# A conv-attention and mixture-of-experts kernel: one tap spread for all images, and tn made twice instead of stored

## The reference, cut to what matters

```python
# 1. attention weights from a 7x7 convolution (dilation 2) of the normalised image
k = relu(conv(ln_c(x), w1, dilation=2, padding=6) + b1)
attn = softmax(relu(batchnorm(conv1x1(k, w2) + b2)), axis=1)       # 49 taps per pixel
# 2. attend: each pixel is the weighted sum of its 49 neighbours, the same for all channels
x = x + sum(attn[:, p] * shifted(ln_c(x), p) for p in range(49))
# 3. a mixture of experts on the tokens t of x, routed by image
t = tokens(x); tn = layernorm(t)
w, i = top2(routing(mean(tn, axis=1)))                              # two of eight experts per image
y = sum(w[k] * (gelu(tn @ W1[i[k]] + b1) @ W2[i[k]] + b2) for k in 2)
out = t + layernorm(y + tn) * gamma + beta
```

## Time and profile before

| | us |
|---|---|
| median of three runs | 1263.26 (1258.61 to 1263.72) |
| profiled execution | 1263.83 |
| its span | 1261.9 |
| PE busy | 1128.5 (89%) |
| PEld busy | 981.5 (78%) |
| DVE busy | 714.7 (57%) |
| ACT busy | 494.8 (39%) |
| POOL busy | 236.2 (19%) |
| mean granted clock of PE | 0.896 |
| DMA | 106.34 MB, 84 GB/s |

### The profile page before, as it was taken

One profiled execution on the slowest core, in us unless ns is written; L12 is line 12 of the kernel. 1 busy time (PEld: TensorE's weight loads), 2 busy tenths in 40 slices (PEclk: granted clock), 3 DMA queues, 4 the chain that ended last, 5 costly groups with the idle time before them and its releaser, 6 DMA issues. The chain is left out here.

```text
span 1261.9 us, 19335 instructions
## 1 busy us (share of the span) xinstructions
PE 1128.5 (89%) x7380; PEld 981.5 (78%) x7380; DVE 714.7 (57%) x1719; ACT 494.8 (39%) x923; POOL 236.2 (19%) x160
## 2 busy tenths in 40 slices
PE   4788999999999999578779887699899989989997
PEld 3776666666667665378779887699899989989997
DVE  3554453554454252335754674667677667777676
ACT  4573323323322110132543443645545535445442
POOL 1000000000000000100440462213233222232332
PEclk9788999999999999556775785799999989999999
DMA  9311121022020000233990685423124221421211
GB/s 256 106 38 38 38 75 39 1 86 80 1 65 27 1 12 4 52 85 86 253 270 3 169 244 177 130 71 107 50 76 126 70 70 50 137 75 42 71 51 38
DMA packets 98968, 106.34 MB, mean 84 GB/s; under 512 B 5298, under 2 KB 95699, under 8 KB 98692
## 3 DMA queue, kind: packets, MB, share of 16 engines
q1 hardware_dynamic: 79888, 86.15, 24.0%
q10 hardware_dynamic: 19000, 19.11, 5.0%
HBM read 65.69 MB, written 39.56 MB: 83 GB/s over the span
## 5 line engine op out<-in xcount | busy, mean ns | idle before, releaser
L706 PE MATMUL pM<-V,U 128*128 128x368 f16 (+3 forms) x2016 | 320.9, 316 | 0.0
L706 PEld LDWEIGHTS pM<-V,U 128*128 128x128 f16 x2016 | 197.3, 98 | 108.2 <-issue 1.6
L1473 DVE TENSOR_TENSOR gl<-gf,gh 128x384 fp32r<-128x384 f32 x192 | 161.8, 864 | 63.4 <-ACT gh L1367 63.4
L1367 ACT ACTIVATE gf<-pH,b1c 128x384 f32<-128x384 f32 x192 | 112.1, 584 | 195.3 <-PE pH L1586 146.3
L1601 PE MATMUL pY<-w2h,gh 128*128 128x256 f32 x576 | 168.6, 293 | 17.3 <-DVE z L1485 16.4
L1601 PE MATMUL pY<-w2l,gh 128*128 128x256 f32 x576 | 164.1, 285 | 0.0
L1601 PE MATMUL pY<-w2h,gl 128*128 128x256 f32 x576 | 164.0, 285 | 0.0
L510 DVE TENSOR_TENSOR V<-pV,V 128x384 f16<-128x384 f32 x96 | 53.1, 554 | 164.9 <-ACT V L408 164.9
L1586 PE MATMUL pH<-xh,w1h 128*128 128x384 f32 x384 | 131.7, 343 | 8.5 <-DVE w1l L1444 4.2
L1586 PE MATMUL pH<-xl,w1h 128*128 128x384 f32 x384 | 131.2, 342 | 0.0
L1586 PE MATMUL pH<-xh,w1l 128*128 128x384 f32 x384 | 131.0, 341 | 0.0
(11 more groups left out here) (173 smaller groups left out, 1544.7 us busy)
## 6 DMA issues: line engine op xcount, KB each, us to landing
xa<-in_xt SPq DMA_DIRECT2D x16, 576.0 KB, 4.9
xn_scratch<-xa SPq DMA_DIRECT2D x16, 576.0 KB, 5.9
xn<-xn_scratch SPq DMA_DIRECT2D x16, 576.0 KB, 8.7
xr<-in_xt SPq DMA_DIRECT2D x16, 576.0 KB, 6.8
t_scratch<-ts ACTq DMA_DIRECT2D x16, 576.0 KB, 5.6
tn_scratch<-tn ACTq DMA_DIRECT2D x16, 576.0 KB, 5.2
tnk<-tn_scratch SPq DMA_DIRECT2D x24, 384.0 KB, 3.3
tk<-t_scratch SPq DMA_DIRECT2D x24, 384.0 KB, 3.9
```

What stands on the lines that cost most here:

```text
L706: return nc.tensor.matmul(out[:, :, first:end], U[:, hi_u, k, piece, :], V[:, b % 2, hi_v, k, c, :, first + TILES * d:end + TILES * d], st ...
L1367: last = nc.scalar.activation(dst, pH[:, j % 4, 0:CN], ACT.Gelu, bias=b1c[:, j // FB, j % FB:j % FB + 1])
L1473: tt(gl[:, sl, j, :], gf[:, j % 2, :], gh[:, sl, j, :].bitcast(F32), ALU.subtract).then_inc(g_step, 1)
```

## The change

Attend is rebuilt. Blocks are five rows of the image instead of four (`BROWS`; `TB` = 120 tokens, five blocks, the last of 96), which makes 13 (t, d) pairs x 3 = 39 matmuls an image. High and low taps are stacked on 98 partitions, and one spread fills A for all 16 images: 11 (d, h) pairs x 4 slots of six matmuls, each with 80 columns (64 where h = 4). The bank holds the sum of both halves: ACT copies it to A's high half, DVE subtracts that to get the low half. X has three buffers, tn isn't stored, and the order on DVE, ACT and SP is another. In the FFN only t is loaded (six buffers, four chunks ahead), and tn is made again: `statistics` on DVE, `scale_x` on POOL, `normalise` on ACT.

```diff
+BROWS = 5
+TB = BROWS * SIDE
+HHS = [(d, h) for d in (-1, 0, 1) for h in range(BROWS) if h - R < BROWS * (d + 1) and h + R >= BROWS * d]
+SLOT = 6
+XB = 3
+SBANKS, OBANKS = 3, 4
...
-        aT = sb("aT", [TAPS, 2, GI * PIX], F16)
-        A = sb("A", [TT, BLK, 2 * BT, TT], F16)
+        aT = sb("aT", [2 * TAPS, N], F16)
+        A = sb("A", [TB, BLK, 2, IMGS, NB, TB], F16)
...
 (SP, attend; halves() cuts each transfer in two: four blocks of 120, one of 96)
             def load_x(n):
                 if n >= 2:
                     sp.wait_ge(t_step, (n - 2) * T_STEPS + T_SUMS)
-                sp.dma_start(xr[:, n % 2], src).then_inc(xr_loaded[n % 2], 16)
+                for src, dst in halves(xt, n, xr[:, n % 2]):
+                    sp.dma_start(dst, src).then_inc(xr_loaded[n % 2], 16)
+            for hl in range(2):
+                sp.dma_start(aT[hl * TAPS:(hl + 1) * TAPS, :], attn_d[:, hl, :]).then_inc(at_loaded, 16)
...
+            for n in range(2, IMGS):
+                load_xn(n)
+                load_x(n)
...
 (POOL, attend)
+            for a in range(2):
+                nc.gpsimd.memset(A[:, 0, a, :, :, R * SIDE:TB], 0.0).then_inc(a_zeroed, 1)
+                nc.gpsimd.memset(A[:, 2, a, :, :, 0:(BROWS - R) * SIDE], 0.0).then_inc(a_zeroed, 1)
...
 (ACT, attend)
+            def store(n):
+                act.wait_ge(t_step, n * T_STEPS + T_SUMS)
+                for dst, src in halves(t_d, n, ts_[:, n % 2]):
+                    act.dma_start(dst, src).then_inc(t_stored[n % 2], 16)
-                act.dma_start(tn_d[rows, :].rearrange("(t p) c -> p t c", p=TT),
-                              tn[:, n % 2]).then_inc(tn_stored[n % 2], 16)
+            for u in range(NU):
+                act.wait_ge(spread, u + 1)
+                nc.scalar.copy(spread_to(0, u), spread_from(u)).then_inc(ahi_spread, 1)
+                if u in (NU // 3, 2 * NU // 3):
+                    x_high(u // (NU // 3) - 1)
             for n in range(IMGS):
+                if n + 2 < IMGS:
                     x_high(n + 2)
                 if n > 0:
+                    store(n - 1)
                     normalise(n - 1)
-                    store(n - 1)
...
 (DVE, attend)
+            for u in range(NU):
+                dve.wait_ge(ahi_spread, u + 1)
+                nc.vector.tensor_tensor(spread_to(1, u), spread_from(u), spread_to(0, u), ALU.subtract).then_inc(alo_spread, 1)
             for n in range(IMGS):
+                if n + 2 < IMGS:
+                    x_low(n + 2)
                 sums(n)
-                if (n + 1) % GI > 0:
-                    statistics(n)
-                    if n + 2 < IMGS:
-                        x_low(n + 2)
+                statistics(n)
...
 (PE, attend)
+                if u >= SBANKS:
+                    pe.wait_ge(alo_spread, u - SBANKS + 1)
+                for w in range(k * SLOT, (k + 1) * SLOT):
...
+                    last = nc.tensor.matmul(pS[0:TB, u % SBANKS, o:o + IMGS * nb], G[:, v, at:at + TB],
+                                            aTv[:, :, first:first + (nb - 1) * TB + 1:TB], start=True, stop=True)
...
 (FFN)
+TBUFS = CHUNKS
+X_STEPS = 2 * CT + 2
+AHEAD = 4
...
-                sp.dma_start(tnk[:, s], tn_d[rows, :].rearrange("(t p) c -> p t c", p=P)).then_inc(tnk_loaded[s], 16)
...
 (POOL, FFN: in step m scale_x(m+3) stands ahead of add_bias(m+1))
+            def scale_x(b, m):
+                n, s = CHUNKS * b + m, m % 2
+                pool.wait_ge(x_step, (n + 1) * X_STEPS)
+                if not (is_first(b) and m < 2):
+                    pool.wait_ge(tn_made, 2 * (n - 1))
+                nc.gpsimd.tensor_tensor(xrs[:, s], xve[:, s], mhalf[:, :], ALU.pow).then_inc(x_scaled, 1)
+                pool.wait_ge(x_scaled, 2 * n + 1)
+                nc.gpsimd.tensor_tensor(xsh[:, s], xnm[:, s], xrs[:, s], ALU.mult).then_inc(x_scaled, 1)
...
 (ACT, FFN: in step m normalise(m+3) stands between gelus(m+1) and take_x(m+2))
+            def normalise(b, m):
+                n, s = CHUNKS * b + m, m % 2
+                act.wait_ge(x_scaled, 2 * (n + 1))
+                if not (is_first(b) and m < 2):
+                    act.wait_ge(x_turned, 2 * (n - 1))
+                    act.wait_ge(bias_added, 2 * (n - 1))
+                for t in range(CT):
+                    last = nc.scalar.activation(tnk[:, s, t, :], tk[:, m % TBUFS, t, :], ACT.Identity,
+                                                bias=xsh[:, s, t:t + 1], scale=xrs[:, s, t:t + 1])
+                last.then_inc(tn_made, 2)
...
+            normalise(0, 0)
+            normalise(0, 1)
             take_x(0, 0)
...
 (DVE, FFN: in step m statistics(m+3) stands ahead of everything else)
+            def statistics(b, m):
...
+                for t in range(CT):
+                    s.did(nc.vector.bn_stats(xst[:, t, :], tk[:, m % TBUFS, t, :]))
...
+                for t in range(CT):
+                    s.did(nc.vector.bn_aggr(xmv[:, t, :], xst[:, t, :]))
...
+                s.did(nc.vector.tensor_scalar(xve[:, sl], xmv[:, :, 1], 1e-5, None, ALU.add))
+                s.did(nc.vector.tensor_scalar(xnm[:, sl], xmv[:, :, 0], -1.0, None, ALU.mult))
```

More of the change, by code:

```diff
@@ L955, in _, with spread_to, spread_from @@
                 scale(n)
-                if n % BI != 1 and 0 < n <= IMGS - LATE:
+                if n % BI != 1 and n > 0:
                     accumulate(n - 1)
[L959 to L972, removed]
+            accumulate(IMGS - 1)
+        def spread_to(hl, u):
+            d, h, k = ITEMS[u]
+            at = h * SIDE + k * SLOT
+            return A[:, d + 1, hl, :, 0:blocks_of(h), at:at + SLOT]
+        def spread_from(u):
+            nb = blocks_of(ITEMS[u][1])
+            return pS[0:TB, u % SBANKS, 0:SLOT * IMGS * nb].rearrange("p (w n t) -> p n t w", w=SLOT, t=nb)
         @block.scalar
@@ L986, in normalise @@
                 if n >= 2:
-                    act.wait_ge(tn_stored[n % 2], 16 * (n // 2))
                     act.wait_ge(acc_step, summed(n - 2))
[L990 to L993, removed]
-                last.then_inc(tn_ready, 1)
[L996 to L1000, removed]
-                act.dma_start(tn_d[rows, :].rearrange("(t p) c -> p t c", p=TT),
-                              tn[:, n % 2]).then_inc(tn_stored[n % 2], 16)
+                else:
+                    act.wait_ge(pads_set, 4 + n)
@@ new lines, in normalise @@
+                for t in range(NB):
+                    rows = rows_of(t)
+                    last = nc.scalar.activation(tn[0:rows, n % 2, t, :], ts_[0:rows, n % 2, t, :], ACT.Identity,
+                                                bias=shift[0:rows, n % 2, t:t + 1],
+                                                scale=rstd[0:rows, n % 2, t:t + 1])
+                last.then_inc(tn_ready, 1)
+            for u in range(NU):
[3 more added lines that the diff above has]
+                    x_high(u // (NU // 3) - 1)
@@ L1042, in statistics @@
                 s.settle()
-                for t in range(NT):
-                    s.did(nc.vector.bn_stats(st[:, t, :], ts_[:, n % 2, t, :]))
+                for t in range(NB):
+                    rows = rows_of(t)
+                    s.did(nc.vector.bn_stats(st[0:rows, t, :], ts_[0:rows, n % 2, t, :]))
                 s.settle()
-                for t in range(NT):
-                    s.did(nc.vector.bn_aggr(mv[:, t, :], st[:, t, :]))
+                for t in range(NB):
+                    rows = rows_of(t)
+                    s.did(nc.vector.bn_aggr(mv[0:rows, t, :], st[0:rows, t, :]))
                 s.settle()
@@ L1527, in body @@
                 for m in range(CHUNKS):
+                    if later(b, m, 3, CHUNKS):
+                        statistics(*later(b, m, 3, CHUNKS))
                     if m == 0 and not is_first(b):
```

310 lines of the change are left out of this document (159 added, 151 removed).

## The result

The changed kernel took 1342.72 us (median of four runs, 1335.85 to 1344.74) against 1260.93 us before (four runs, 1256.41 to 1263.72): a ratio of 1.0643, with a 95% interval of 1.0588 to 1.0698. It is slower by 82 us. The forecast was 1379, with a range of 1300 to 1420. The profiled execution took 1340.77 us, its span is 1339.0 us and its mean granted clock 0.881.

A forecast was written before the change was run, and what follows sets the result against it. It took attend as seemingly bound by bytes, the FFN chunk by PE and the DVE/ACT chain. Terms: 1263.8 + 4 (attend) + 5 (FFN head) + 71 (chunk waits) + 35 (clock) = 1379 us; range 1300 to 1420.

The forecast's parts named there:

- The sign: Whole kernel: slower by over 0.5%, chance 0.89; within 0.5%, 0.04; faster, 0.07.
- the clock holds: Rival, FFN: PE's waits do not lower its clock, total 1344 us (band 1330 to 1350); chance 0.17.
- Head of attend: Attend's start until the first spread matmul: 22.5 us, 9 longer than the 13.5 before, for the larger load.
- The case at the upper end: Attend's head: both tap transfers of 49 rows share seven DMA engines, 2.4 us more than the 9 taken.
- Spread: Spread of the taps: 264 matmuls at 0.173 us at the low clock, 47 us with the last copies, 35 saved.
- Ring: Attend loop: xn load, x_high, x_low and sums wait in a closed circle, 12.2 us an image, 13 turns, 159 us.
- the ring gives back what was saved: Attend: the closed ring eats what spread and stores save, so the stage ends 4 us later, at 786.5.
- bytes decide: Rival, attend: bytes, not order, set 7.2 us an image, 65 us less; FFN chunks add nothing; 1208 us; faster, chance 0.07.
- FFN head: Start of the FFN: tn must be made before the first layer-1 matmul, 5 us more (bounds 3 and 9).
- FFN chunks: FFN loop: statistics and normalise in the chain cost 3.4 us a chunk, 71 us over 21, plus 35 for the clock.
- the clock falls after every such wait: FFN: after PE's wait ahead of the third group, matmuls run partly at low clock, 1.7 us a chunk, 35 us altogether.
- only statistics counts: Rival, FFN: POOL's wait is met already, only statistics lengthens the chain, 21 x 1.3 = 27 us; 1300 to 1310; chance 0.12.

The follow-up runs named there:

- e4: Changed kernel with each load of 49 tap rows cut into 48 rows and one row, same bytes: 1343.7 us, ratio 1.064.
- both attend edits: Changed kernel with both FFN orders mended, SP asking for xn one image earlier and DVE doing x_low last: 1195.8 us, ratio 0.949.
- e5: Changed kernel with ACT's normalise(m+3) in the FFN moved behind take_x(m+2) and split_w1: 1287.2 us, ratio 1.021.
- e6: Changed kernel with DVE's FFN statistics (of chunk m+4) moved into sum_up, where DVE waits for PE: 1318.4 us, ratio 1.045.
- e7: Both FFN orders: changed kernel with ACT's normalise put later and DVE's statistics moved into sum_up: 1260.3 us, ratio 0.999.

## Why the prediction was right, and where its terms were off

The sign, both mechanisms and their places were right; the sum was 36 us too high. The time did not fall into the forecast's own bounds (1350 to 1420, chance 0.52) but just below them, into the band given to the rival "the clock holds" (1330 to 1350, 0.17). Against the profiled execution the forecast was 38 us too high: 12 of them lie in attend, 1 in the head of the FFN and 24 in its chunks.

**Head of attend: 22.5 forecast, 16.7 measured.** The term of 9 us for the larger load was too large; it was 3.2. I took it between the price of the bytes alone (5.6 us) and that of a second transfer that only follows the first (11.4); the lower was nearer and still too high. The whole wait moved 202 GB/s here (the row is beside e4), against 183 over the 13.5 us before, where I had priced the added bytes alone at 214:

```profile
529.00:542.50 13.50, 0.00 (x0) 0.01 (x1) 0.00 (x0) 0.00 (x0) 4.05 (x4) 0.50 0.89 183
```

The case at the upper end went by a rule of the Trainium skill (a transfer uses the largest number of engines up to 16 that divides its outermost size, so 7 for 49 rows and 16 for 48), "DMA: Bandwidth & Descriptors", section on why a DMA increments its semaphore by 16. The landing doesn't bear it out here: loads of 48 rows should have been faster by it, and were not (e4). The higher busy share of the DMA engines in that run may come from it; no view shows the engines singly.

**Spread: 47 forecast, 43 measured.** The copies took 0.56 and 0.66 us, as worked out. A matmul took 43 / 264 = 0.163 us, not 0.173: taking it in proportion to the columns was a little too much. The clock stayed at 0.50, the lower level (1.2 GHz), with PE busy for 97% of the 43 us. That is against the rule of the Trainium skill, "TensorE: Matmul & The Clock Gate", Part 1, that sustained busy matmuls get the full clock; the measurement decides, as it did for the spread of before.

**Ring: 12.2 forecast, 11.6 measured.** Thirteen turns (`sums` of image 0 end at 596.7, of image 13 at 747.7) took 151 us instead of 159. The landing was 7.5 us instead of 7.8, and neighbours overlap by some 0.1 us where I had added 0.1. The first image took 7.7 (7), the last two 12.2 (8; PE's 39 matmuls of the last one alone took 6.1), the tail 14.6 (14). All told 529.2 + 16.7 + 43 + 7.7 + 151 + 12.2 + 14.6 = 774.4 where the forecast had 786.5. The statement that the ring gives back what was saved was right for most of it: attend came out 8 us shorter than before, not 4 us longer, and it would have been far shorter without the ring, since with both attend edits a turn takes 6.96 us. So 13 x 4.7 = 61 us, near the 65 that the rival "bytes decide" had named, lay in the order alone.

**FFN head: 5 forecast.** The first layer-1 matmul comes 17.1 us after the stage's start (791.6 against 774.5), before 13.5: 3.6 us.

**FFN chunks: 106 forecast (71 for the waits, 35 for the clock), 82 measured**, between the first chunk's add(2) and the 22nd's: 479.3 us (826.95 to 1306.23) against 397.5 before (831.59 to 1229.05). Before the first of them lies one more wait, of 1.56 us only, which cost nothing beyond the 3.6 of the head. By kind of step:

| step | number | before, mean | after, mean | longer | forecast |
|---|---|---|---|---|---|
| plain | 14 | 17.97 | 21.74 | 3.8 | 5.1 |
| with the w1 split | 3 | 22.86 | 26.15 | 3.3 | 4.7 |
| with the w2 split | 3 | 19.82 | 26.16 | 6.3 | 5.1 |
| last | 1 | 17.87 | 17.96 | 0.1 | |

In the plain steps the shortest is 20.72, so the wait alone costs 2.75 us instead of 3.4. The chain forecast 18.3 us from add(2) to PE's start; in the chunk above it is 17.9, since `finish` moved by 1.0 instead of 1.3 and neighbouring instructions overlap. What is over 20.72 comes to 14.3 us in 14 steps, 1.0 us each; the forecast had 1.7. Here the step "the clock falls after every such wait" failed in part: eight of the fourteen lost 1.2 us or more, six lost 0.3 or less. Two neighbouring chunks (PE alone), and then the first 4.4 us behind the wait in each:

```profile
1106.66:1127.70 21.04, 17.76 (x128) 1.00 0.45 139
1127.70:1149.93 22.23, 19.08 (x127) 0.93 0.14 46
1124.55:1129.00 4.45, 4.45 (x33) 1.00 0.85 255
1145.50:1149.90 4.40, 4.40 (x25) 0.65 0.00 2
```

The first wait was 3.28 us and the clock stayed at 1.00; the second was 3.15 us and it fell to 0.65. The length of the wait doesn't tell them apart: the shortest of the 14, 2.54 us, lost the clock too (0.61 over the next 4.4 us). The rival "the clock holds" was therefore half right, and its 1344 is close to the result by luck: its other terms were too high by about what the clock loss, which it left out, took.

The steps with the w2 split were forecast too cheap. There the statistics, 1.8 us, stand ahead of `split_w2`, and PE waits 1.4 to 4.7 us ahead of layer 1 as well; with the statistics moved as well (both FFN orders) these steps take 19.8, 22.6 and 19.5 us. In the middle one DVE further stood 3.12 us with nothing shown that it waited for:

```profile
1084.85 0.06 DVE L100 MEMSET spare<- 1x1 f32 x1 [3.12 <-issue]
```

The rival "only statistics counts" was wrong: without ACT's wait (e5) the kernel is 56 us faster, without the statistics' place (e6) 24, and with both (e7) 82. The two shares overlap by nothing that can be measured (56 + 24 = 80). The shift of the statistics alone is worth 0.8 us a plain chunk (18.8 with ACT's order mended, 18.0 with both), where the forecast had 1.3.

**What stays open.** Why a wait of 3.3 us keeps the clock in one chunk and one of 3.15 us loses it in the next; why the tap load took 16.7 us, whole or cut; why the spread never gets the full clock; and what DVE stands for in the middle w2 split (it does so too with both FFN orders mended, 2.97 us; before the change 0.48 us at that place). Apart from e4 on the tap load, no experiment was made on these.

## What to carry to other kernels

Before saving bytes or instructions, write down for each loop the ring of waits that goes once around (load issue, landing, each engine's step, the step that allows the next issue) and price it; a piece of work on an engine that is 30% busy costs its full length if it stands in that ring, and nothing a few lines later. Work that waits for a late engine belongs behind everything that others wait for in the same queue. A load that can go early must not stand behind one that has to wait.

## What the runs showed of the hardware

- 264 matmuls in a row with PE busy for 97% of 43 us ran at the lower clock (0.50) from the first to the last, while matmuls of the FFN hold 0.98.
- Waits of 2.5 to 3.3 us on PE cost the clock in eight plain chunks of 14, and not by their length: 3.28 us kept it, 3.15 us lost it (0.65 over the next 4.4 us), and so did 2.54 us (0.61).
- A transfer of 49 rows and one cut into 48 + 1 rows, with the same bytes ahead of the same wait, landed after the same 16.7 us, while the busy share of the DMA engines rose from 0.67 to 0.94 and the larger parts of the loads of xn beside it landed later (16.3 us after issue instead of 9.6).
- With two loads of 480 + 96 KB an image and the stores beside them, DMA reached 258 GB/s at a share of 0.91.
